# An attention, feed-forward and routing kernel: another order in the first layer with floors and key scaling on GpSimd, the widest scores computed by rows, and the second layer's output norm weight folded away with the routing in three parts

## The chip, the cores and the metric

The kernel is one program on one core of a Trainium2 chip. The metric is the device time of one execution in microseconds. Before the change it is 578.08 us, the median of 3 runs (577.95 to 581.03).

## The reference

The input `x` is 16 batches of 128 tokens of 128 features, all fp32. Two layers are added to it in turn. Cut to what matters:

```python
# layer 1: cosine attention, 16 heads of 64 queries, one head of keys and values, a learned null key
xn = ln(x, g_norm)
q = l2norm(xn @ Wq) * q_scale                      # l2norm floors the norm
k = l2norm([null_k ; (xn @ Wkv)[:, :64]]) * k_scale
v = [null_v ; (xn @ Wkv)[:, 64:]]
sim = 8 * q @ k.T + rel_pos_bias                   # causal and masked by key
x = x + ffn(ln(softmax(sim) @ v @ Wout, g_out))    # dense FFN: ln, ternary W1, gelu, ln, ternary W2
# layer 2: the same shape of attention without l2norm, with a bias given as input
h = ln(softmax(q @ k.T + bias) @ v @ Wo, g_out)
logits = h @ gate_w.T + gate_b                     # 8 experts
p, idx = top_k(softmax(logits), 2)
# each choice c: token t goes to row idx*320 + (its place among the tokens of that expert), dropped from 320 on
y[t] = sum over c of p[t,c] * keep[t,c] * (relu(xbuf[e] @ W1[e] + b1[e]) @ W2[e] + b2[e])
x = x + y
```

## The kernel before, in words

The program is written by hand, engine by engine: each of PE, ACT, DVE, POOL and SP has its own list of instructions, and semaphores order them across engines. There is no scheduler: on an engine, what stands first waits first, and everything behind it waits too. `over` walks the 16 batches in pairs (some batches written out, the rest in a loop); `attention_first` is the walk of layer 1 and `attention_second` that of layer 2, once for each engine.

A batch's 128 queries are four units of 32. Unit `u` needs only the keys up to its own end: 33, 65, 97 and 129 columns with the null key. For a unit and a batch PE multiplies queries by keys (`scores`, L888), DVE adds bias and mask and takes the negated row maximum (`biased`, L1590, four instructions, one for each pair of heads), ACT takes the exponential and the row sum (`weights`, L1296, four), DVE divides (`divide`, L1599 and L1605), PE turns the probabilities (`turn_pair` L895 and L897 for units 0 and 1, `turn_probs` L906 for 2 and 3), ACT copies them out of PSUM (`pair_T` L1303, `weights_T` L1309), and PE multiplies them by the values (`values_pair` L914 and L915 for units 0 and 1; `values` L924 for units 2 and 3, in column tiles of 128 rows by 64 columns, two side by side). DVE copies the result out (`outputs`, L1617), and PE projects it (`project`, L943, 8 matmuls). Scores lie in `psS`, two banks, each unit but the last in one; unit 3 takes both banks, 258 columns in each:

```python
if u == UNITS - 1:
    return psS[:, 1 - h, 0:2 * w]
```

Its second matmul waits until DVE has read unit 2. Both matmuls have 128 rows: the keys `kk` hold the 64 rows of a head twice, padded with zeros, so that two heads share a matmul.

In layer 1 the queries and keys of the next batch are made meanwhile: PE projects (`project_values` L838, `project_heads` L843), ACT squares (`squares`, L1263 for the keys, L1265 for the queries), DVE sums (`sum_squares`), floors (`floored`, L1576), POOL takes the power -1/2 (L584, output `qrn`), DVE scales keys (`keys_in`, L1563) and queries (`queries_norm`, L1581), PE turns them (`turn_keys` L866, `turn_queries` L872, half 0 and 1), ACT copies them back (`queries` L1279, `keys_T` L1289 and L1290). POOL also adds bias and mask for the next batch (`mask_bias`, L637) and the null value (`values_set`, L620).

In layer 2 each batch ends in the output norm: DVE reads `psA` (`out_stats` L1624, `out_read` L1638), POOL gives the reciprocal root, DVE centres and scales 136 columns, the 128 of the token and 8 raw logits (`centre` L1654 and L1656, `rescale` L1661). Groups of tokens (`GROUPS`: most batches, then two, then the last three) are routed: logits (`route_logits`, L1898), exponential (ACT, L1387), the two largest (`route_top`, L1909 to L1915), shares (`route_share`, L1923 to L1927), positions by matmul on PE (`positions`, L954) and slots (`route_slots`, L1935 to L1945). POOL scatters each tile's rows by an indirect DMA (`scatter`, L649), two of a tile, into two slot arrays. SP loads the slots of the first two experts when both arrays are complete (`load_slots`, L485), and the experts run.

## Time and profile before

| | |
|---|---|
| median of 3 runs | 578.08 us |
| the profiled execution | 581.05 us |
| its span in the trace | 579.3 us |
| mean granted clock of TensorE | 0.938 of full speed |
| busiest engine | PE, 84% of the span |

The profiled execution is the slowest of those shown, 3.0 us above the median. In the trace, the layer-1 attention runs from about 45 to 218 us, the dense feed-forward to 267, the layer-2 attention to 450, the last scatters and loads to 472, the experts to 555, the return of their rows to the end. A row of the timeline is a run of instructions on one engine: start, time to the end of the last, engine, line, operation, tiles, count, and in brackets the idle time ahead of it with what ended it. A row of the chain is a piece of the chain of work that ended last: start, time, what. A row by form is a group of instructions: count, busy time and mean ns of one, then the idle time ahead of them with what ended it. A row by stretch gives the stretch and its length, then busy time (and instructions) of PE, PE's weight loads, DVE, ACT and POOL, the granted clock, the DMA share and GB/s.

### The profile page before, as it was taken

The numbers are of one execution on the slowest core, as the hardware profiler recorded it, in microseconds if no ns is written. First come the engines' busy times: TensorE is split into PE (matmuls) and PEld (weight loads), VectorE is DVE, ScalarE is ACT, GpSimd is POOL, SyncE is SP. The second block draws the span as 40 slices with busy tenths as digits, with TensorE's granted clock in tenths as the row PEclk, the third lists the DMA queues.
The fourth block names the chain that finished last, engine by engine and source line by source line (L and its number), as shares of the span: only waits on it lengthen the run. The fifth ranks groups of instructions, "written<-read, shape, count | busy, mean of one in ns | idle before, by whom it ended". The sixth has DMA issues, their size and how long they took to land.

```text
span 579.3 us, 13792 instructions
## 1 busy us (share of the span) xinstructions
PE 485.3 (84%) x3220; PEld 391.4 (68%) x3220; DVE 422.1 (73%) x2148; ACT 375.2 (65%) x1475; POOL 303.6 (52%) x368
## 2 busy tenths in 40 slices
PE   2778999999999889979899999989778139999930
PEld 1456777777777676758688888868666127878730
DVE  3889999999999896877978888887796503343413
ACT  1568889888888876747798888967763004344410
POOL 4486666665646724775353343425766512555650
PEclk9779999999999999989999999999978759999975
DMA  5451016721100000000111210000111121323117
GB/s 166 97 182 24 20 26 130 152 78 44 43 5 5 9 4 2 0 1 9 45 42 44 79 42 8 5 6 21 33 39 40 36 64 36 85 56 83 35 39 217
DMA packets 54696, 29.73 MB, mean 51 GB/s; under 512 B 19884, under 2 KB 51572, under 8 KB 54644
## 3 DMA queue, kind: packets, MB, share of 16 engines
q1 hardware_dynamic: 48900, 22.09, 15.6%
q0 software_dynamic: 2560, 4.90, 2.7%
q10 hardware_dynamic: 3184, 2.16, 1.2%
q8 instruction: 18, 0.29, 0.2%
q14 instruction: 34, 0.28, 0.2%
HBM read 16.13 MB, written 10.90 MB: 47 GB/s over the span
## 4 chain that ended last, share of the span: by engine, by line
PE 58%; issue 11%; DVE 9%; POOL 7%; ACT 7%; DMA 5%; SPq 1%; ACTq 0%; DVEq 0%; POOLq 0%
PE psS L888 10%; PE psA L943 8%; PE psS L1193 6%; PE psT L906 5%; PE psO L924 4%; PE psQ L843 4%; PE psQ L859 4%; PE psQ L1183 3%; ACT sc L1296 2%; PE psO L914 2%; DVE sc L1590 2%; PE psO L915 2%; DMA slot_rows<-Y,dest_u 2%; ACT qT L1279 2%; PE psA L1183 1%
## 5 line engine op out<-in xcount | busy, mean ns | idle before, releaser
L1296 ACT ACTIVATE sc<-sc,negmax 128x97 f32<-128x97 f32 (+3 forms) x512 | 179.0, 354 | 26.0 <-DVE negmax L1590 25.5
L637 POOL TENSOR_TENSOR wide_buf<-bias,mask 128x132 f32<-128x132 f32 (+3 forms) x128 | 100.2, 799 | 97.5 <-DVE pn L1605 84.0
L888 PE MATMUL psS<-kk,qT 128*128 128x194 f32 (+3 forms) x512 | 102.1, 321 | 7.9 <-DVE negmax L1590 7.8
L1590 DVE CUSTOM_DVE_ANT_0 sc<-psS,wide_buf 128x97 f32<-128x97 f32 (+3 forms) x512 | 93.6, 238 | 17.5 <-PE psS L888 13.1
L888 PEld LDWEIGHTS psS<-kk,qT 128*128 128x128 f32 x512 | 79.6, 194 | 28.6 <-issue 25.1
L1296 ACT ACTIVATION_READ_ACCUMULATOR sc<-sc,negmax 128x1 f32 x512 | 97.6, 191 | 0.0
L584 POOL TENSOR_TENSOR qrn<-qssc,half 128x9 f32<-128x9 f32 (+1 forms) x32 | 55.5, 1735 | 41.8 <-DVE qssc L1576 41.7
L1605 DVE TENSOR_TENSOR pn<-sc,rsum 128x128 f32<-128x128 f32 (+3 forms) x128 | 64.9, 507 | 6.0 <-DVE rsum L1599 0.2
L943 PE MATMUL psA<-Wo,OT 128*128 128x128 f32 (+1 forms) x512 | 66.4, 285 | 0.8 <-DVE OT L1617 0.8
L943 PEld LDWEIGHTS psA<-Wo,OT 128*128 128x128 f32 x512 | 63.8, 199 | 1.8 <-DVE OT L1617 1.2
L1617 DVE TENSOR_SCALAR OT<-psO,cols 128x512 f32<-128x512 f32 x64 | 47.6, 744 | 2.6 <-PE psO L924 1.8
L906 PE MATMUL psT<-ident,pn 128*96 128x128 f32 (+1 forms) x256 | 39.8, 279 | 11.6 <-issue 10.9
L906 PEld LDWEIGHTS psT<-ident,pn 128*96 128x96 f32 (+1 forms) x256 | 28.4, 137 | 25.0 <-issue 24.6
L1590 DVE DVE_READ_ACCUMULATOR2_ANT negmax<- 128x1 f32 x512 | 41.8, 82 | 0.1
L1309 ACT COPY PT<-psT 96x512 f32<-96x512 f32 x64 | 36.7, 573 | 7.6 <-PE psT L906 7.0
L779 POOL DMA_INDIRECT choice_rows<-hT,tags x24 | 22.5, 939 | 35.5 <-ACT hT L1441 23.1
L649 POOL DMA_INDIRECT slot_rows<-Y,dest_u x32 | 32.1, 1005 | 16.2 <-DMA slot_rows<-Y,dest_u 7.5
L843 PE MATMUL psQ<-Wq,xnT 128*128 128x512 f32 x64 | 37.1, 668 | 1.0
L1279 ACT ACTIVATE qT<-psQ 128x512 f32<-128x512 f32 x64 | 34.7, 588 | 3.6 <-PE psQ L872 3.2
L924 PE MATMUL psO<-PT,vp 96*64 96x256 f32 (+1 forms) x256 | 34.8, 392 | 2.5 <-issue 1.5
L2025 DVE TENSOR_SCALAR hm<-psQ,cols 128x320 f32<-128x320 f32 x16 | 8.8, 551 | 35.0 <-PE psQ L1183 35.0
L779 POOL DMA_INDIRECT choice_rows<-qn,tags x24 | 22.5, 939 | 16.6 <-DMA choice_rows<-qn,tags 7.2
(298 smaller groups left out, 1009.7 us busy)
## 6 DMA issues: line engine op xcount, KB each, us to landing
slot_rows<-empty SPq DMA_DIRECT2D x2, 1390.0 KB, 10.5
xb<-slot_rows SPq DMA_DIRECT2D x16, 139.0 KB
vp_u<-vp SPq DMA_DIRECT2D x128, 8.0 KB, 1.7
choice_rows<-zero_row SPq DMA_DIRECT2D x8, 256.0 KB, 3.1
wide_buf<-choice_rows SPq DMA_DIRECT2D x8, 256.0 KB, 5.2
vp_u<-vp SPq DMA_DIRECT2D x64, 16.0 KB, 1.8
eW<-in_L_ffn_W SPq DMA_DIRECT2D x4, 256.0 KB, 3.0
gT<-in_L_ffn_W SPq DMA_DIRECT2D x4, 256.0 KB, 3.3
```

The lines of the kernel that those rows point to most:

```text
L584: pool.tensor_tensor(dst, src, half[:, 0:k], ALU.pow).then_inc(done, count)
L637: pool.tensor_tensor(unit_masked(i, u).rearrange("p h e k -> p (h e) k"), unit_bias(layer, u).rearrange("p h e k -> p (h e) k"), mask[laye ...
L843: pe.matmul(psQ[:, h, :], xnT[i][:], Wq[0][:, 512 * h:512 * (h + 1)], start=True, stop=True).then_inc(s["q_psum"], 1)
L888: m = pe.matmul(score_bank(u, h), qT[i][:, h, u].rearrange("p m q -> p (m q)"), kk[i][:, :, 0:w], start=True, stop=True)
L906: m = pe.transpose(psT[0:k, probs_bank(u, i), g * P:(g + 1) * P], pn[u][:, g, :], ident[:])
L924: m = pe.matmul(psO[DH * e:DH * (e + 1), 2 * P * (u - 2):2 * P * (u - 1)], vp[i][0:k, :], PT[u - 1][0:k, :, e, :], start=True, stop=True)
L943: m = pe.matmul(psA[:, Y_AT[layer]:4 * P], OT[i][:, j].rearrange("p u q -> p (u q)"), Wo[layer][:, j, :], start=(j == 0), stop=(j == 7))
L1279: act.activation(qT[i][:, h].rearrange("p u m q -> p m u q"), v, ACT.Copy, scale=1.0 if layer == 0 else DH ** -0.5).then_inc(s["q_ready"], 1)
L1296: m = act.activation(v, v, ACT.Exp, bias=negmax[:, u, g:g + 1], scale=-1.0, accum_out=psum_row[:, u, g:g + 1])
L1590: dve.tensor_tensor_reduce(sc[u][:, h, e, :], score_bank(u, h)[:, e * WIDTH[u]:(e + 1) * WIDTH[u]], unit_masked(i, u)[:, h, e, :], -1.0, - ...
L1605: dve.tensor_tensor(pn[u][:], sc[u][:].rearrange("p h e k -> p (h e) k")[:, :, 1:k + 1], rsum[:, u, :].unsqueeze(2).broadcast_to([P, 4, k] ...
L1617: dve.tensor_scalar(OT[i][:, :, 2 * half_of:2 * half_of + 2, :], v, cols[:, C_VN:C_VN + 1], None, ALU.add).then_inc(s["out_ready"], 1)
```

## The change

1. **Scores of unit 3 by rows, in both layers.** Instead of two matmuls of 128 rows by 258 columns there are four of 64 rows by 129 columns, one for each half of the array's rows and each pair of heads. Their two banks are now told apart by the half (`score_part`), all four wait until unit 2 is read, and DVE and ACT take them in another order (`in_order`).
2. **Layer 1's order.** PE: `project_heads(b + 1, 0)` comes first in a batch, and `turn_queries(b + 1, 0)` moves from the end of batch `b` to a place ahead of its unit 3. ACT: the squares of the next queries come first, the keys' squares are an instruction of their own, and the copies of the queries' halves are apart. DVE: `biased` of unit 3 moves from the next batch to the end of its own.
3. **Floors and keys on GpSimd.** `floored` and `keys_in` leave DVE; POOL floors just ahead of its power. The keys' and queries' weights and the factor 8 become a column `k_col`, by which ACT scales in `keys_T`.
4. **Layer 2's norm.** `centre` and `rescale`, three DVE instructions a batch, become `finish`, two. The weight `g_out` of layer 2 moves into `rows_T` of the experts, as a scale of ACT's copy, and the gate's column sum into its weights ahead of layer 2 (`gate_total`, `gate_centred`).
5. **Routing in three parts.** `route_slots` becomes `route_positions` and `route_slots`, and shares, positions and slots of the first group move to later batches.
6. **GpSimd's late batches.** From batch 12 of layer 2 on, all four `mask_bias` come ahead of the scatters and wait for nothing, and one scatter moves from inside the last batch to behind it.
7. **The end of layer 2.** PE turns and multiplies the last unit ahead of `project` of batch 14, `project` of batch 15 writes into a bank of its own, DVE's order follows, and the loads of slots are split: SP's queue loads the first choice's, ACT's the second's.

Three of the loads that spread a row over all partitions are gone from SP's queue.

```diff
+        def y_at(layer, b):
+            if layer == 1 and no(b, NB - 1):
+                return psS[:, 0, 0:P + EXPERTS]
+            return psA[:, Y_AT[layer]:4 * P]
...
+        def score_part(u, h, e):
             w = WIDTH[u]
             if u == UNITS - 1:
-                return psS[:, 1 - h, 0:2 * w]
-            return psS[:, u % 2, 2 * w * h:2 * w * (h + 1)]
+                return psS[:, 1 - e, w * h:w * (h + 1)]
+            return score_bank(u, h)[:, e * w:(e + 1) * w]
+        def in_order(u):
+            return [(0, 0), (1, 0), (0, 1), (1, 1)] if u == UNITS - 1 else [(0, 0), (0, 1), (1, 0), (1, 1)]
...
# SP, after the second layer's walk
-            for c in range(TOPK):
-                sp.wait_ge(s[f"slots_out{c}"], 16 * NB)
-            load_slots(0, 0)
-            load_slots(1, 1)
+            sp.wait_ge(s["slots_out0"], 16 * NB)
+            load_choice(sp, 0, 0, 0)
+            load_choice(sp, 1, 1, 0)
+            sp.wait_ge(s["slots_out1"], 16 * NB)
...
# POOL
+                apart(pool, (s["ss_step"], 2 * b + h + 1))
+                pool.tensor_scalar(qssc[:, lo:hi], qss[:, lo:hi], 1e-24, None, ALU.max).then_inc(s["q_floor"], 1)
+                pool.wait_ge(s["q_floor"], 2 * b + h + 1)
                 rsqrt(qrn[:, lo:hi], qssc[:, lo:hi], hi - lo, s["rn_ready"])
+            def keys_in(b, i):
+                pool.wait_ge(s["v_read"], b + 1)
+                pool.wait_ge(s["rn_ready"], 2 * b + 1)
+                held(pool, s["kT_psum"], b - 1)
+                pool.tensor_tensor(kd[i][:], kvs[:, 0:DH].unsqueeze(1).broadcast_to([P, 2, DH]),
+                                   qrn[:, 0:1].unsqueeze(2).broadcast_to([P, 2, DH]), ALU.mult).then_inc(
+                    s["k_ready"], 1)
...
             def attention_second():
                 def batch(b, i):
+                    late = isinstance(b, int) and b >= NB - 4
                     if not no(b, NB - 1):
-                        pool.wait_ge(s["probs_ready"], 4 * (b + NB) + 1)
-                        for u in range(UNITS - 1):
+                        if not late:
+                            pool.wait_ge(s["probs_ready"], 4 * (b + NB) + 1)
+                        for u in range(UNITS if late else UNITS - 1):
                             mask_bias(1, b + 1, u, 1 - i)
...
# PE, scores
-                      (s["scores_ready"], 4 * (n - u) if u < 2 else 4 * (n - 1)))
+                      (s["scores_ready"], 4 * (n - u) if u < 2 else 4 * (n - 1) if u == 2 else 4 * n))
+                if u == UNITS - 1:
+                    for h in range(2):
+                        for e in range(2):
+                            rows_of = slice(DH * e, DH * (e + 1))
+                            m = pe.matmul(score_part(u, h, e), qT[i][rows_of, h, u].rearrange("p m q -> p (m q)"),
+                                          kk[i][rows_of, e, 0:w], start=True, stop=True)
...
# PE, end of layer 2
-                project(1, NB - 2, 0, False)
                 turn_probs(B, 3, 1)
                 values(B, 1)
+                project(1, NB - 2, 0, False)
...
# ACT, keys_T
+                    m = act.activation(kk[i][half_of, e, 1:P + 1], psA[half_of, k0:k0 + P], ACT.Copy,
+                                       scale=k_col[half_of, 0:1] if layer == 0 else 1.0)
...
# ACT, a batch of layer 1
-                    queries(0, b, i)
+                    if not last:
+                        squares(b + 1, 0)
+                    queries(0, b, i, (1,))
+                    if not last:
+                        square_keys(b + 1)
                     if not first:
                         pair_T(b - 1, 1 - i)
-                    if not last:
-                        squares(b + 1, 0)
...
                     weights(4 * b + 1, 1)
+                    if not last:
+                        queries(0, b + 1, 1 - i, (0,))
                     weights(4 * b + 2, 2)
...
# DVE
+            def finish(b, i):
                 dve.wait_ge(s["o_rstd"], b + 1)
+                dve.tensor_scalar(Y[:, b, 0:P], Y[:, b, 0:P], o_mv[:, i, 0:1], o_rs[:, i:i + 1], ALU.subtract,
+                                  ALU.mult)
+                dve.scalar_tensor_tensor(lg[:, bass.ds(b, 1), :].rearrange("p t e -> p (t e)"),
+                                         Y[:, b, RAW_AT:RAW_AT + EXPERTS], o_rs[:, i:i + 1], gate_b[:], ALU.mult,
+                                         ALU.add).then_inc(s["n_step"], 1)
...
                     divide(b, 1)
+                    biased(n + 3, 3, i)
...
-                            if u == 3:
-                                route_share(g)
+                        if u == 1 and (no(b, NB - 5) or last):
+                            route_share(1 if last else 0)
                         if u == 2 and no(b, NB - 5):
-                            route_slots(0, 1)
+                            route_positions(0, 1)
                         if u == 1 and last:
-                            route_slots(1, 0)
+                            route_positions(1, 0)
+                        if u == 1 and (no(b, NB - 4) or last):
+                            route_slots(1 if last else 0)
```

What the change moves is seen in the order of the instructions. On PE, in layer 1, from unit 2 of batch 2 to the first turning of batch 3 (`qn` are the normalised queries, `pn` the probabilities, `kd` the keys), the order before is:

```order
L888 MATMUL psS<-kk,qT 128x194 x2
L924 MATMUL psO<-PT,vp 64x256 x4
L888 MATMUL psS<-kk,qT 128x258 x2
L832 MATMUL psA<-ident,xn 128x128
L866 MATMUL psA<-ident,kd 128x128
L872 MATMUL psQ<-ident,qn 128x128 x4
L895 MATMUL psT<-ident,pn 128x128
L897 MATMUL psT<-ident,pn 128x128 x2
L872 MATMUL psQ<-ident,qn 128x128 x4
L838 MATMUL psA<-Wkv,xnT 128x128
L843 MATMUL psQ<-Wq,xnT 128x512
L906 MATMUL psT<-ident,pn 96x128 x4
```

and with the change:

```order
L928 MATMUL psS<-kk,qT 128x194 x2
L906 MATMUL psQ<-ident,qn 128x128 x4
L964 MATMUL psO<-PT,vp 64x256 x4
L923 MATMUL psS<-kk,qT 128x129 x4
L864 MATMUL psA<-ident,xn 128x128
L900 MATMUL psA<-ident,kd 128x128
L935 MATMUL psT<-ident,pn 128x128
L937 MATMUL psT<-ident,pn 128x128 x2
L877 MATMUL psQ<-Wq,xnT 128x512
L906 MATMUL psQ<-ident,qn 128x128 x4
L870 MATMUL psA<-Wkv,xnT 128x128
L946 MATMUL psT<-ident,pn 96x128 x4
```

The first turning of the queries moved ahead of the values, the projection of the heads (128x512) ahead of the second turning, and the wide scores became four narrow ones.

On POOL, in a batch of layer 1, before:

```order
L584 TENSOR_TENSOR qrn<-qssc,half 128x9
L584 TENSOR_TENSOR rstd<-ve,half 128x6
L584 TENSOR_TENSOR qrn<-qssc,half 128x8
L620 TENSOR_TENSOR vp<-kvs,vnull 128x64
L637 TENSOR_TENSOR wide_buf<-bias,mask 128x132
```

and with the change:

```order
L628 TENSOR_SCALAR qssc<-qss 128x9
L598 TENSOR_TENSOR qrn<-qssc,half 128x9
L637 TENSOR_TENSOR kd<-kvs,qrn 128x128
L598 TENSOR_TENSOR rstd<-ve,half 128x6
L628 TENSOR_SCALAR qssc<-qss 128x8
L598 TENSOR_TENSOR qrn<-qssc,half 128x8
L645 TENSOR_TENSOR vp<-kvs,vnull 128x64
L662 TENSOR_TENSOR wide_buf<-bias,mask 128x132
```

Two floors and the keys' product joined POOL's list, each ahead of a power or of the values.

On PE, at the end of layer 2, behind the last scores, before:

```order
L906 MATMUL psT<-ident,pn 96x128 x4
L914 MATMUL psO<-PT,vp_u_1 128x128 x2
L915 MATMUL psO<-PT,vp_u_1 128x256
L943 MATMUL psA<-Wo,OT 128x136 x8
L906 MATMUL psT<-ident,pn 128x128 x4
L924 MATMUL psO<-PT,vp 64x256 x4
```

and with the change:

```order
L946 MATMUL psT<-ident,pn 96x128 x4
L954 MATMUL psO<-PT,vp_u_1 128x128 x2
L955 MATMUL psO<-PT,vp_u_1 128x256
L946 MATMUL psT<-ident,pn 128x128 x4
L964 MATMUL psO<-PT,vp 64x256 x4
L984 MATMUL psA<-Wo,OT 128x136 x8
```

The projection of batch 14 moved behind the last batch's turning and values.

## Rows read from the trace of the kernel before

**Rows 1.** Busy time of each engine, layer 1 from the first projection to the last.
```profile
56.41:205.51 149.10, 145.10 (x945) 110.85 (x944) 136.21 (x713) 129.20 (x555) 94.03 (x103) 1.00 0.23 50
```

**Rows 2.** Chain that ended last, layer 1, the first and the last projection.
```profile
56.41 1.79 PE psA L943 x16
...
205.51 1.79 PE psA L943 x16
```

**Rows 3.** PE's timeline, one batch of layer 1.
```profile
101.55 0.63 PE L906 MATMUL psT<-ident,pn 128*128 128x128 f32 x4
...
107.76 0.60 PE L872 MATMUL psQ<-ident,qn 128*128 128x128 f32 x4
...
108.81 1.12 PE L843 MATMUL psQ<-Wq,xnT 128*128 128x512 f32 x2
...
113.17 0.63 PE L906 MATMUL psT<-ident,pn 128*128 128x128 f32 x4 [0.16 <-issue]
```

**Rows 4.** ACT's timeline in the same batch.
```profile
108.15 1.09 ACT L1279 ACTIVATE qT<-psQ 128x512 f32<-128x512 f32 x2
109.12 0.49 ACT L1303 COPY PT<-psT 128x384 f32<-128x384 f32 x1
...
109.97 0.60 ACT L1265 ACTIVATE qsq<-psQ 128x512 f32<-128x512 f32 x1 [0.23 <-PE psQ L843]
110.46 0.39 ACT L1296 ACTIVATE sc<-sc,negmax 128x129 f32<-128x129 f32 x1
...
112.00 0.56 ACT L1309 COPY PT<-psT 96x512 f32<-96x512 f32 x1
```

**Rows 5.** Chain that ended last: layer 1 by its first three rows, then layer 2.
```profile
104.63 1.01 PE psO L924 x8
105.65 1.07 PE psS L888 x4
...
111.71 0.86 PE psQ L843 x2
...
375.75 0.26 PE psA L832
376.02 0.87 PE psS L888 x4
376.89 0.11 PE psT L895
```

**Rows 6.** POOL's groups by form, whole span.
```profile
L584 POOL TENSOR_TENSOR qrn<-qssc,half 128x9 f32<-128x9 f32 x16 | 28.8, 1803 | 8.6 <-DVE qssc L1576 8.6
...
L637 POOL TENSOR_TENSOR wide_buf<-bias,mask 128x132 f32<-128x132 f32 x32 | 15.9, 498 | 41.3 <-DVE pn L1605 39.5 <-issue 1.8
```

**Rows 7.** DVE's groups by form, whole span.
```profile
L1590 DVE CUSTOM_DVE_ANT_0 sc<-psS,wide_buf 128x129 f32<-128x129 f32 x128 | 29.6, 285 | 5.4 <-PE psS L888 5.3
...
L1661 DVE TENSOR_SCALAR Y<-centred,o_rs 128x136 f32<-128x136 f32 x10 | 5.6, 558 | 0.1
...
L1563 DVE SCALAR_TENSOR_TENSOR kd<-kvs,qrn,kqs 128x128 f32<-128x128 f32 x16 | 5.4, 340 | 0.1
...
L1576 DVE TENSOR_SCALAR qssc<-qss 128x9 f32<-128x9 f32 x16 | 3.1, 197 | 0.1
```

**Rows 8.** DVE's timeline, layer 2, the batch behind the first scatters.
```profile
405.65 0.23 DVE L1556 COPY kvs<-psA 128x64 f32<-128x64 f32 x1 [1.90 <-POOL vp L620]
```

**Rows 9.** PE's timeline, end of layer 2, the projection of batch 14.
```profile
442.79 3.45 PE L943 MATMUL psA<-Wo,OT 128*128 128x136 f32 x16
```

**Rows 10.** DVE's timeline, end of layer 2, the last group's two largest.
```profile
447.45 0.31 DVE L1909 MAX8 top<-le 128x8 f32<-128x8 f32 x3 [2.11 <-ACT le L1387]
```

**Rows 11.** POOL's timeline, the first and the last of the last ten scatters.
```profile
452.62 1.03 POOL L649 DMA_INDIRECT slot_rows<-Y,dest_u  x1 [1.81 <-DVE Y L1945]
...
465.53 0.96 POOL L649 DMA_INDIRECT slot_rows<-Y,dest_u  x1 [0.30 <-DMA slot_rows<-Y,dest_u]
```

**Rows 12.** SP's queue, the loads of the first two experts' slots.
```profile
467.98 4.50 SPq L485 DMA_DIRECT2D xb<-slot_rows  x8
```

More of the change, by code:

```diff
@@ L1260, in squares, with square_keys, queries @@
                 held(act, s["ss_step"], 2 * b)
[L1261 to L1263 removed]
                 act.wait_ge(s["q_psum"], 2 * b + h + 1)
[L1265 to L1268 removed]
+                m = act.activation(qsq[:, 1 + 8 * h:9 + 8 * h, :], psQ[:, h, :].rearrange("p (h d) -> p h d", d=DH),
+                                   ACT.Square)
+                if h:
+                    m.then_inc(s["sq_ready"], 1)
+            def square_keys(b):
+                act.wait_ge(s["kv_psum"], b + 1)
+                act.activation(qsq[:, 0, :], psA[:, P:P + DH], ACT.Square).then_inc(s["sq_ready"], 1)
+            def queries(layer, b, i, halves=(0, 1)):
                 B = b + NB * layer
                 held(act, s["scores_psum"], 4 * B - 4)
[L1271 removed]
+                for h in halves:
                     if layer == 0:
@@ L1328, in batch @@
                     weights(4 * b + 1, 1)
+                    if not last:
+                        queries(0, b + 1, 1 - i, (0,))
                     weights(4 * b + 2, 2)
@@ L1344, in attention_first @@
                 ternary_abs()
+                input_T(0, 1, 1)
+                queries(0, 0, 0, (0,))
                 keys_T(0, 0, 0)
-                input_T(0, 1, 1)
                 over(act, NB, batch, 2, 2)
@@ L1691, in batch @@
                         outputs(b - 2, 1, i, True)
-                    if not first:
-                        biased(n - 1, 3, 1 - i)
                     if first:
@@ L1717, in batch @@
                         out_stats(0, b - 2, i)
-                    if not last:
-                        floored(b + 1, 1)
                     biased(n + 2, 2, i)
@@ L1722, in batch @@
                         moments(b - 2, i)
-                    if not last:
-                        keys_in(b + 1, 1 - i)
-                    else:
+                    if last:
                         dense_stats(1)
```

204 lines of the change are left out of this document (96 added, 108 removed).

## The prediction

> **What bounds the kernel now.** I read the busy time by stretch first. In layer 1, from the first projection to the last, PE is busy 145.1 of 149.1 us, DVE 136.2, ACT 129.2 and GpSimd 94.0, at the full clock [rows 1]. PE sets the pace, DVE (91%) stands close behind, and GpSimd has a third to spare. The chain of waits says how long a batch is: the first and the last of its projections lie 149.1 us apart [rows 2], which is 13 batches of 11.47 us.
>
> Then I read one batch on PE and on ACT. PE turns unit 2 at 101.55, the queries' second half at 107.76 and unit 3 at 113.17 [rows 3]: two parts of 6.21 and 5.41 us. In the second part ACT works with 0.23 us of waiting: it copies the queries' halves from 108.15, the pair from 109.12, squares from 109.97, takes unit 3's exponentials from 110.46, and copies unit 2's turned probabilities from 112.00 [rows 4]. ACT alone would hold that part at its length. That decides the largest term below.
>
> Late in layer 2 the reading changes: DVE waits for GpSimd, which scatters ahead of the next values [rows 8], and behind the last scores the chain runs through the routing, ten scatters and the first loads of slots [rows 9 to 12].
>
> **The scores by rows.** No row of this trace has matmuls of 64 rows. The nearest are the column tiles of the values: eight records of 256 columns in 1.01 us [rows 5], where the scores, four full records of 258 columns, take 0.87 in layer 2 [rows 5]. Eight at that price would be 1.74, so the column tiles run two at a time. A record of 128 columns takes 0.11 (the turning at 376.89). What goes into another tile mode costs more: the scores take 1.07 behind column tiles, 0.20 more than the 0.87 behind a full matmul, and the input's turning behind column tiles takes 0.26, not 0.11, so 0.15 [rows 5]. The new visit has eight records of 129 columns. Side by side that is 4 x 0.11 + 0.20 + 0.15 = 0.79, say 0.80: 0.27 less in layer 1, 0.07 less in layer 2. One after another it is 8 x 0.11 + 0.35 = 1.23; with a weight load of the same length ahead of each it is 8 x 0.22 + 0.35 = 2.11. I take side by side, as the column tiles show it. All four now wait until DVE has read unit 2; before, only the second matmul did. Behind them on PE stand the turnings of the input, the keys and the pair, and for these ACT waits; the values ahead of the scores (1.01) cover the wait.
>
> The Trainium skill's page "TensorEngine Tiling (Array Packing)", under Key Properties, says that different tiles load and multiply in parallel, and that a change of mode drains the engine. By the first half the visit is the 0.80 above, by the second both switches are paid, and the sum stands; no run here shows it for tiles of rows yet.
>
> **Layer 1's order.** The second part has PE waiting at the projection of the heads: 1.12 us [rows 3], against 0.86 for the same two matmuls where nothing waits [rows 5]. The new order projects the heads first and takes that 0.26 away. But ACT's list is as long as it was. From the moment the heads are there: squares 0.49 (109.97 to 110.46), the queries' half 0.49 (half of the 0.97 from 108.15 to 109.12), pair and key squares 0.62 (109.12 to 109.74), exponentials of unit 3 1.54 (110.46 to 112.00), and 1.17 from there to PE's turning [rows 3, 4]. With 0.86 + 0.23 (the projection and ACT's wait behind it) ahead, that is 5.40, as the 5.41 before. So this part keeps its length, and only the first one shrinks: 6.21 - 0.27 = 5.94. Moving the turning of the queries and biasing unit 3 earlier lets ACT start its exponentials a little sooner; for that I add 0.08, an estimate between nothing and the 0.23 of ACT's wait [rows 4]. A batch loses 0.35, and 13 batches **-4.6**. The bounds are 0 (PE waits for what it gained) and -13 (1.0 a batch: 0.27, the 0.26, and the two 0.23 waits of ACT, once each for both parts).
>
> **Floors and keys on GpSimd.** DVE loses 2 x 0.20 and 0.34 a batch [rows 7]. GpSimd gains them: nearest rows are its sum of 132 columns, 0.50, and its power of 9 columns, 1.80 [rows 6]. Two floors at 0.2 to 1.8 and a product of 0.50 make 0.9 to 4.1 a batch; GpSimd had 55.1 us free in 13 batches [rows 1], 4.2 each. Beside other work in either case: **0**. The chain from the sums to the turned keys gets longer by 0.2 to 1.8, and the keys are turned at the end of the batch.
>
> **Start and end of layer 1.** Three loads and two products go from the setup, one column joins: 0, give or take 1. At the end unit 3's bias of batch 15, four of about 0.28 [rows 7], less what it already overlaps, comes ahead of the last divide: **+0.7**, between 0 and 1.1.
>
> **Layer 2, ten batches.** PE gives 0.07 a batch. DVE's norm drops one of three instructions, the one of 0.56 [rows 7]; DVE is not the bound, so I count 0.08 of it. -0.15 each, **-1.5**, between 0 and -3.5 (the 0.07 and half of the 0.56).
>
> **Late batches.** DVE waits 1.90 for GpSimd's values behind four scatters [rows 8], and once more like it a batch later. In the new list the masks go ahead of the scatters without waiting, so scatters and values start sooner; the scatters themselves take as long. Shares and slots leave the batch that is fullest. I take 3.0 of the 3.8 us: **-3.0**, between -1 and -4.5 (both waits and 0.7 for the routing that moved).
>
> **The end.** PE projects batch 14 for 3.45 us [rows 9] ahead of the last turning; now it doesn't. DVE waits 2.11 for the exponential of the last routing, as ACT takes it behind unit 3's work [rows 10]. With the unit turned sooner, the first of the ten scatters, at 452.62 [rows 11], comes between 2.1 and 3.45 sooner; their pace, 12.9 us for nine steps [rows 11], does not change. I take 2.8. The eight loads take 4.50 us on one queue [rows 12], 0.56 each; over two queues the first expert's four are out two steps sooner, up to 1.1; I take 0.6. Together **-3.4**, between -2.1 and -4.6. ACT issues its four behind the last exponential, and behind them on ACT stand only the copies that need the loaded rows. The experts keep their price: a copy with a scale for a copy.
>
> **Sum.** -4.6 + 0.7 - 1.5 - 3.0 - 3.4 = -11.8. The profiled execution took 581.05 us (span 579.3), so 569.25; the median of the runs is 578.08, 0.5% below it, which gives 566.3, **566 us**. About 0.5% (2.9 us) is what a measurement of this kernel can tell from no change.
>
> **The rivals** (all against the median).
>
> - *ACT gives way and PE alone bounds layer 1.* The batch loses 1.0, 8.4 us more than forecast over 13 batches: 558. For it: the new order feeds ACT earlier. Against it: ACT had only 0.23 of waiting there [rows 4], and its work is the same.
> - *DVE sets the pace of layer 1.* It was busy 136.2 of 149.1 [rows 1], and loses 0.74 a batch; if the places where it must answer PE (unit 2 read ahead of all four scores, where before the first of two didn't wait) eat the gain, layer 1 stands where it was: 4.6 less gain, 571. The Trainium skill's same page, under PSUM Bottleneck, says that tiling speeds up TensorE but not the emptying of PSUM; by that rule this rival would be the forecast. The rows speak for it with DVE's 91% and against it with the 0.74 that leave DVE.
> - *The row tiles run one after another.* A visit is 1.23: layer 1 then gains 0.08 - 0.16 = 0.08 worse a batch (+1.0), layer 2 loses 0.36 - 0.08 = 0.28 a batch (+2.8); with the rest, +1.0 + 0.7 + 2.8 - 3.0 - 3.4 = -1.9: 576, no change that can be told.
> - *The slower side: weight loads stand open between the row tiles.* Each of the eight records waits for its own load, 2.11 a visit. Layer 1 loses 2.11 - 1.07 - 0.08 = 0.96 a batch (+12.5), layer 2 2.11 - 0.87 - 0.08 = 1.16 (+11.6), and with the other terms +19.1: 597. It turns to slower as soon as a visit costs over about 1.35. For it: PE's loads were busy 110.9 us of layer 1 [rows 1], so they are not far from the matmuls. Against it: the column tiles, with as many loads, show none of it [rows 5].
> - *The change does not do what it says.* A wait put wrongly could keep the old order in time; the order of the instructions shows it done.
>
> **Chances.** Forecast 0.54 (its own range 561 to 571, from the bounds of the sum), PE alone 0.12, DVE 0.15, one after another 0.10, open loads 0.08, nothing changed 0.01. The range 555 to 576 leaves out the open loads, the slower half of the tiles one after another and the edges of the first three. Faster: the first three, less 0.02 for the third, 0.79. Same: tiles one after another, the 0.02 and the 0.01, 0.13. Slower: 0.08.
>
> **What would show it.** Right: projections of layer 1 about 11.1 apart; the four narrow scores starting in pairs and taking about 0.8 with their switches; the heads at 0.86; the waits of 1.90 at the values' copy gone; the first of the last ten scatters about 3 us nearer to the last scores. Wrong: the distance still 11.47, with PE waiting at unit 3's scores for DVE (the second rival), or the eight records following each other by 0.11 (the third) or 0.22 (the fourth); or powers on GpSimd ending after PE has reached the keys' turning, which would price the floors above the range.

## The result, and the profile after

The changed kernel takes 583.42 us (median of 6 runs, 580.84 to 586.44), the kernel before 578.10 in the same set: the ratio is 1.0077, 95% interval 1.0048 to 1.0105. It is slower by 0.8% where 2% faster was forecast, and outside the range. The profiled execution took 586.44, the slowest of the six (span 584.7); differences of stages below are taken against the profiled execution before (581.05, span 579.3), which was also the slowest of its runs. Medians below leave out one run in the slower state in each of three versions (594.95, 728.47 and 634.80 us).

Layer 1 in the changed kernel, by busy time from the first projection to the fourteenth (as in [rows 1]), and the chain there (as in [rows 2]):

```profile
56.12:207.86 151.74, 141.98 (x996) 108.44 (x996) 131.66 (x675) 131.75 (x555) 105.44 (x142) 1.00 0.21 49
```

```profile
56.12 1.79 PE psA L984 x16
...
207.86 1.79 PE psA L984 x16
```

PE has 3.1 us less work than before and DVE 4.5 less, ACT has 2.5 more, and the same 13 batches take 151.74 us instead of 149.10. The busiest engine, PE, is now idle for 9.8 us where it was for 4.0: no engine is full, and a ring of waits over several engines sets the pace (a ring: each waits for the one ahead of it, and the first for the last). PE's timeline of one batch shows where PE stands (as in [rows 3]):

```profile
94.82 0.72 PE L923 MATMUL psS<-kk,qT 64*128 64x129 f32 x8
95.47 0.33 PE L864 MATMUL psA<-ident,xn 128*128 128x128 f32 x1
...
96.59 1.12 PE L877 MATMUL psQ<-Wq,xnT 128*128 128x512 f32 x2 [0.36 <-ACT xnT L1302]
97.55 0.60 PE L906 MATMUL psQ<-ident,qn 128*128 128x128 f32 x4
...
99.09 0.63 PE L928 MATMUL psS<-kk,qT 128*128 128x66 f32 x4 [0.28 <-ACT qT L1329]
```

The scores by rows do run side by side: eight records in 0.72 us where 0.80 was forecast; in the trace they start in pairs, 0.01 us apart in a pair and 0.11 from pair to pair. They do not wait for DVE here. But the heads, now first in the batch, wait for ACT's copy of the input, and unit 0's scores wait for ACT's copy of the queries. The chain of the same batch shows why the copy of the input is late:

```profile
92.78 0.68 PE psS L928 x4
...
94.73 1.23 ACT sc L1352 x7
...
96.08 0.38 ACT xnT L1302
96.46 0.14 issue
96.59 1.14 PE psQ L877 x2
...
98.25 0.60 ACT qT L1329
```

From unit 2's scores the chain goes over DVE's bias to ACT's exponentials of unit 2 (`sc`), and the copy of the input (`xnT`) stands behind these. Neither unit 3's scores nor the copies of the keys stand in the chain, in this batch or anywhere from 56 to 208 us.

Late in layer 2 three timelines (DVE, GpSimd, PE) belong together:

```profile
410.68 0.23 DVE L1621 COPY kvs<-psA 128x64 f32<-128x64 f32 x1 [2.17 <-POOL vp L645]
...
411.60 3.00 DVE L1656 TENSOR_TENSOR pn<-sc,rsum 128x512 f32<-128x512 f32 x1
```

```profile
404.97 1.24 POOL L674 DMA_INDIRECT slot_rows<-Y,dest_u  x1 [3.06 <-DVE Y L1987]
...
410.24 0.34 POOL L645 TENSOR_TENSOR vp<-kvs,vnull 128x64 f32<-128x64 f32 x1
...
411.07 2.98 POOL L662 TENSOR_TENSOR wide_buf<-bias,mask 128x132 f32<-128x132 f32 x4
```

```profile
414.70 1.09 PE L946 MATMUL psT<-ident,pn 128*128 128x128 f32 x4 [3.57 <-issue]
415.58 3.83 PE L984 MATMUL psA<-Wo,OT 128*128 128x136 f32 x16
```

A wait for GpSimd's values is still there (2.17, as in [rows 8]); the second one, a batch later, is gone. The scatters ahead of these values did not start sooner, as the first of them waited 3.06 us for DVE's slots. Then DVE's division of 512 columns takes 3.00 us: it ends at 414.60, 0.55 behind the last of GpSimd's four mask sums. PE stands 3.57 us, and then its clock is granted at half (1.2 GHz; the mean of the stretch from 410 to 430 is 0.83 of full speed): the projection takes 3.83 where it takes 2.02 at full clock.

The same fall of the clock stands at the start of layer 2, where before there was none, behind the longer wait of unit 3's scores (PE's timeline, before and after):

```profile
283.27 0.67 PE L888 MATMUL psS<-kk,qT 128*128 128x258 f32 x2 [1.15 <-DVE negmax L1590]
...
285.02 1.95 PE L859 MATMUL psQ<-xnT,Wq 128*128 128x128 f32 x16
```

```profile
288.25 1.23 PE L923 MATMUL psS<-kk,qT 64*128 64x129 f32 x8 [1.57 <-DVE negmax L1641]
...
290.96 3.60 PE L893 MATMUL psQ<-xnT,Wq 128*128 128x128 f32 x16
```

The end of layer 2 does what was forecast (as in [rows 10, 11], DVE, GpSimd and PE):

```profile
452.70 0.30 DVE L1948 MAX8 top<-le 128x8 f32<-128x8 f32 x3 [0.29 <-ACT le L1449]
```

```profile
458.35 1.03 POOL L674 DMA_INDIRECT slot_rows<-Y,dest_u  x1 [0.45 <-DVE Y L1987]
...
471.31 0.95 POOL L674 DMA_INDIRECT slot_rows<-Y,dest_u  x1 [0.30 <-DMA slot_rows<-Y,dest_u]
```

The wait of 2.11 is 0.29. The last scores of unit 3 begin at 445.85 and the ten scatters 12.5 us behind them; before it was 437.75 and 14.9.

**Where the time went**, by the starts of the projections in PE's timeline, before and after (us):

| stretch | before | after | difference |
|---|---|---|---|
| start to the first projection | 56.25 | 55.95 | -0.3 |
| 13 batches of layer 1 | 149.09 | 151.75 | +2.7 |
| its last two projections | 15.59 | 18.20 | +2.6 |
| feed-forward, to layer 2's first projection | 68.90 | 71.17 | +2.3 |
| eight batches of layer 2 | 82.23 | 81.12 | -1.1 |
| the batch with the first routing | 12.98 | 11.07 | -1.9 |
| four late batches | 47.79 | 52.04 | +4.2 |
| from there to the end | 146.5 | 143.4 | -3.1 |

### The profile page after: what moved, and what is told of

It reads as the page before. It is cut to its first block, busy times and chain, and to the rows that moved or that the text cites. A ratio compares the mean times of both kernels' runs of the same rounds, so it can differ in the third digit from the quotient of the medians.

```text
span 584.7 us, 13956 instructions
## 1 busy us (share of the span) xinstructions
PE 486.0 (83%) x3348; PEld 391.6 (67%) x3348; DVE 408.5 (70%) x2073; ACT 381.5 (65%) x1475; POOL 318.9 (55%) x416
## 4 chain that ended last, share of the span: by engine, by line
PE 60%; issue 10%; DVE 9%; ACT 8%; DMA 5%; POOL 5%; SPq 1%; DVEq 0%; ACTq 0%; POOLq 0%
PE psA L984 9%; PE psS L928 8%; PE psS L1240 6%; PE psQ L877 5%; PE psT L946 5%; PE psQ L893 4%; ACT sc L1352 4%; PE psQ L1230 3%; DVE sc L1641 3%; PE psO L954 3%; PE psO L964 2%; PE psO L955 2%; PE psS L923 2%; DMA slot_rows<-Y,dest_u 2%; PE psA L1230 1%
## 5 line engine op out<-in xcount | busy, mean ns | idle before, releaser
L662 POOL TENSOR_TENSOR wide_buf<-bias,mask 128x132 f32<-128x132 f32 (+3 forms) x128 | 98.8, 794 | 89.7 <-DVE pn L1656 85.7
L928 PE MATMUL psS<-kk,qT 128*128 128x130 f32 (+2 forms) x384 | 66.9, 296 | 8.1 <-DVE negmax L1641 4.2
L1656 DVE TENSOR_TENSOR pn<-sc,rsum 128x128 f32<-128x128 f32 (+3 forms) x128 | 67.3, 526 | 5.8
L928 PEld LDWEIGHTS psS<-kk,qT 128*128 128x128 f32 x384 | 57.7, 194 | 20.0 <-issue 19.2
L984 PE MATMUL psA<-Wo,OT 128*128 128x128 f32 (+1 forms) x496 | 65.2, 287 | 0.0
L984 PEld LDWEIGHTS psA<-Wo,OT 128*128 128x128 f32 x496 | 62.1, 200 | 0.6 <-issue 0.4
L598 POOL TENSOR_TENSOR qrn<-qssc,half 128x9 f32<-128x9 f32 (+1 forms) x32 | 56.9, 1778 | 2.7
L946 PE MATMUL psT<-ident,pn 128*96 128x128 f32 (+1 forms) x256 | 41.1, 285 | 10.3 <-issue 9.1
L1365 ACT COPY PT<-psT 96x512 f32<-96x512 f32 x64 | 36.9, 576 | 15.8 <-PE psT L946 14.9
L1329 ACT ACTIVATE qT<-psQ 128x512 f32<-128x512 f32 x64 | 36.0, 588 | 13.9 <-PE psQ L906 13.8
L893 PE MATMUL psQ<-xnT,Wq 128*128 128x128 f32 x256 | 32.8, 284 | 0.0
```

Source lines behind the costliest of these rows:

```text
L598: pool.tensor_tensor(dst, src, half[:, 0:k], ALU.pow).then_inc(done, count)
L662: pool.tensor_tensor(unit_masked(i, u).rearrange("p h e k -> p (h e) k"), unit_bias(layer, u).rearrange("p h e k -> p (h e) k"), mask[laye ...
L893: m = pe.matmul(psQ[:, h, j * P:(j + 1) * P], Wq[1][:, (4 * h + j) * P:(4 * h + j + 1) * P], xnT[i][:], start=True, stop=True)
L928: m = pe.matmul(score_bank(u, h), qT[i][:, h, u].rearrange("p m q -> p (m q)"), kk[i][:, :, 0:w], start=True, stop=True)
L946: m = pe.transpose(psT[0:k, probs_bank(u, i), g * P:(g + 1) * P], pn[u][:, g, :], ident[:])
L984: m = pe.matmul(y_at(layer, b), OT[i][:, j].rearrange("p u q -> p (u q)"), Wo[layer][:, j, :], start=(j == 0), stop=(j == 7))
```

## The experiments

All ratios are to the kernel before, run on the same chip in the same set, with 95% intervals. The first set undoes one part each, and does one alone.

**Mask waits back.**

```diff
-                    late = isinstance(b, int) and b >= NB - 4
+                    late = False
```

> The changed kernel with one thing undone: in layer 2's batches from 12 on, GpSimd's mask sums wait again for the division of the unit ahead and stand on both sides of the scatters. Theory: without those waits the sums (2.98 us at 411.07) run beside DVE's division of the same time, which took 3.00 us where it takes 0.69, PE then stood 3.57 us and ran 6.8 us at half clock; with the waits back the division takes about 0.7 everywhere, the low clock there goes, and 4 to 6 us come back: 578 to 579. Rival: the division was slow for another reason, or the scatters merely wait elsewhere: 582 to 584.

580.57 us, 1.0035 (1.0012 to 1.0057). In its DVE timeline the division of the same batch takes 0.69 again:

```profile
410.54 0.69 DVE L1656 TENSOR_TENSOR pn<-sc,rsum 128x512 f32<-128x512 f32 x1
```

PE's wait ahead of the turning is 1.09, and the low clock at 414 is gone: four late batches take 45.23 instead of 52.04. The collision is shown, though the run gained 2.9 us by the medians, 2.4 by the ratios, and not 4 to 6. The Trainium skill's page "SBUF — State Buffer", under Who interferes with whom, says that a DVE instruction with two inputs in SBUF contends with a GpSimd instruction that reads SBUF, over ports that only one of them holds at a time; the 3.00 beside the 2.98 agree, and I had not weighed that section.

**Old order, with the rest of the change.** PE, ACT and DVE of layer 1 as before:

```diff
-                    if not last:
-                        project_heads(b + 1, 0, 1 - i)
                     turn_queries(b, 1)
                     if not last:
                         project_values(b + 1, 1 - i)
+                        project_heads(b + 1, 0, 1 - i)
...
                     divide(b, 1)
-                    biased(n + 3, 3, i)
...
```

> The changed kernel with layer 1's order undone on PE, ACT and DVE (heads, queries' turning, squares, copies and the bias of unit 3 where they were before); floors and keys stay on GpSimd and the scores by rows stay. Theory: the new order puts the queries' copy ahead of unit 2's exponentials on ACT and the heads behind the input's copy, and gives back what the scores by rows gain; undone, a batch of layer 1 takes about 11.2 instead of 11.65 us, 13 batches 5 to 6, and the end of layer 1 starts without a fall of the clock: 576 to 578. Rival: floors on GpSimd or the wait for unit 2 hold layer 1; then a batch stays above 11.5 and the time at 583.

588.25 us, 1.0163 (1.0115 to 1.0211): slower still, so my theory fell. A batch takes 11.89. (This undo left the keys' squares behind the queries' on ACT, which was not so before.)

**Full scores, with the rest of the change.**

```diff
-                        for e in range(2):
-                            rows_of = slice(DH * e, DH * (e + 1))
-                            m = pe.matmul(score_part(u, h, e), qT[i][rows_of, h, u].rearrange("p m q -> p (m q)"),
-                                          kk[i][rows_of, e, 0:w], start=True, stop=True)
+                    m = pe.matmul(bank, qT[i][:, h, u].rearrange("p m q -> p (m q)"),
+                                  kk[i][:, :, 0:w], start=True, stop=True)
...
```

> The changed kernel with the scores of unit 3 again as two matmuls of 128 rows, of which only the second waits for unit 2. Theory: a visit by rows takes 0.65 us instead of 1.07 to 1.16, so without it PE is busy 0.4 longer in layer 1 and 0.2 to 0.4 in layer 2; as layer 1 is now held by ACT's order, only part shows: 584 to 589. Rival: waiting for all of unit 2 costs what the rows save (PE stood 1.57 at the start of layer 2 and lost its clock); then 580 to 583.

585.98 us, 1.0103 (1.0069 to 1.0136), as the theory had it. A batch takes 11.95: in the new order the rows are worth 0.28 a batch.

**Rows alone, on the kernel before.**

> The kernel before with one part of the change: the scores of unit 3 by rows, in both layers. Theory: side by side a visit takes about 0.65 instead of 1.07 in layer 1 and 0.87 in layer 2; a batch of layer 1 loses 0.3 to 0.45 and one of layer 2 0.1 to 0.2: 571 to 574. Rival: the wait of all four matmuls for unit 2 eats it, as DVE stands close behind PE: 577 to 580, with PE waiting for DVE ahead of these scores.

579.63 us, 1.0014 (0.9991 to 1.0037): the rival. Its chain in a batch of layer 1:

```profile
103.72 0.68 PE psS L903 x4
...
105.51 0.09 DVE negmax L1606
105.61 0.14 issue
105.74 0.72 PE psS L898 x8
```

From the end of unit 2's scores (104.40) to that of unit 3's (106.46) it takes 2.06 us; before, from 104.63 to 106.72 [rows 5], 2.09. PE's timeline has the scores wait 0.34 for DVE's last read of unit 2. The 0.35 that the rows save (0.72 for 1.07) goes into that wait. In layer 2 eight batches take 10.20 each instead of 10.28.

A second set took the floors back to DVE, once in the new order and once in the old, and made only half of the scores wait for unit 2.

**Floors on DVE, new order, mask waits back.**

```diff
-                pool.tensor_scalar(qssc[:, lo:hi], qss[:, lo:hi], 1e-24, None, ALU.max).then_inc(s["q_floor"], 1)
...
+                dve.tensor_scalar(qssc[:, lo:hi], qss[:, lo:hi], 1e-24, None, ALU.max).then_inc(s["q_floor"], 1)
...
```

> The changed kernel with GpSimd's mask waits back (as in the first run, 580.57 us) and, beyond that, floors and the keys' scaling back on DVE; layer 1's new order and the scores by rows stay. Theory: with the old order, scores by rows and floors on DVE a batch of layer 1 takes 11.4 us, with floors on GpSimd 11.83, so the move to GpSimd costs 0.4 a batch in the chain from the sums to the normalised queries, and the new order gives half of it back; with floors on DVE the new order shows its gain: a batch about 11.2, 13 batches 5 to 6 less: 575. Rival: in the new order the batch is a ring of heads, squares, exponentials, division and projection that holds neither floors nor keys; then it stays at 11.6 and the time at 580 to 581.

579.60 us, 1.0021 (0.9997 to 1.0045), a batch of 11.64 against 11.67: the rival. Floors and keys on GpSimd cost nothing that can be told, as forecast.

**Old order and floors on DVE** (the two undos together, mask waits back).

> The changed kernel without its layer 1 parts: old order, floors and keys on DVE, mask waits back. What stays of the change is the scores by rows, the norm folded in layer 2, the routing in three parts and the end of layer 2. Theory: layer 1 as in the run with the scores by rows alone (11.4 a batch), the first scatters' batch about 1.9 shorter, the end about 2.7 shorter: 579.63 less 4 to 5, so 575. Rival: the feed-forward between the layers and the falls of the clock behind it take that back: 578 to 580.

581.83 us, 1.0050 (1.0023 to 1.0078). A batch stayed at 11.89, though only the column scale on ACT and the place of the keys' squares were left of layer 1's change beside the rows. The time is above both ranges. That pointed to ACT.

**Only half of the scores wait.**

```diff
-                    for h in range(2):
-                        for e in range(2):
+                    for e in range(2):
+                        if e == 1:
+                            apart(pe, (s["scores_ready"], 4 * n))
+                        for h in range(2):
```

> The changed kernel with mask waits back (580.57 us), and the four matmuls of unit 3's scores in another order: both of the upper half's rows first, into the bank that unit 2 does not use, without waiting for unit 2, then both of the lower half's behind the wait. The two halves then no longer run side by side. Theory: where PE waited 1.57 us for unit 2 at the start of layer 2 it waits about 1.1, and its clock falls less often; a visit costs 1.2 instead of 0.65, which layer 1 does not feel, as its batches are not held by PE; layer 2 feels 0.3 to 0.5 in ten batches: 581 to 584. Rival: the falls of the clock hang on that wait more than on anything else: 577 to 579.

579.62 us, 1.0011 (0.9989 to 1.0033), against 580.57: within the spread. A visit in layer 1 still took 0.72, not 1.2, so the halves ran side by side in this order too. At the start of layer 2 PE stood only 0.94 ahead of the second half, and the clock fell all the same (the projection behind it took 3.62). So that one wait's length does not decide the fall.

The third set, with ACT's list restored, led to the version that beats both kernels.

**Old order with the keys' squares first** (scaled copies and GpSimd's floors stay).

> The changed kernel with mask waits back, layer 1's old order, and now also the keys' squares ahead of the queries' on ACT as before; floors and keys stay on GpSimd, and ACT still scales in the copies of the keys (0.36 us each where a plain copy took 0.26). Theory: the 11.8 a batch of the two runs in the old order came from ACT, which squared the keys (0.22) behind its wait for the heads and not within it, and from the scaled copies (0.2 a batch), not from GpSimd: a batch takes about 11.6, 0.2 above the run with the scores by rows alone. Rival: the floors and the keys on GpSimd are late; then it stays near 11.8.

583.15 us, 1.0060 (1.0034 to 1.0087), a batch of 11.79: the rival's number. That floors and keys on GpSimd are its cause is not shown by it; the last pair of runs speaks against that.

**Layer 1 of before with rows; layer 2 changed, with mask waits.**

```diff
-                    m = act.activation(kk[i][half_of, e, 1:P + 1], psA[half_of, k0:k0 + P], ACT.Copy,
-                                       scale=k_col[half_of, 0:1] if layer == 0 else 1.0)
+                act.copy(kk[i][0:DH, 0, 1:P + 1], psA[0:DH, k0:k0 + P])
+                act.copy(kk[i][DH:P, 1, 1:P + 1], psA[DH:P, k0:k0 + P]).then_inc(s["kk_ready"], 1)
```

> Layer 1 of the kernel before, but with the scores by rows, and layer 2 of the changed kernel with mask waits back: floors and keys on DVE with the product of the keys' and queries' weights, plain copies of the keys, old order. Theory: layer 1 takes 11.4 a batch as in the run with the scores by rows alone (579.63), the first scatters' batch is 1.9 shorter, ten batches of layer 2 about 0.15 each, the end about 2.7, less 1 for the scaled copies of the experts' rows: 574 to 576. Rival: the clock falls between the layers and at the end take it back: 578 to 580.

577.57 us, 0.9979 (0.9950 to 1.0009): between the two, and not clear of no change. A batch takes 11.53.

**The same with full scores.**

> As the run with layer 1 of the kernel before and layer 2 of the changed one, but with unit 3's scores as two full matmuls, of which only the second waits for unit 2. Theory: PE is not what holds a batch of layer 1, so the full scores cost nothing there, about 0.1 in each of ten batches of layer 2; and PE's stop of 1.57 at the start of layer 2 becomes 1.15 again, behind which the clock did not fall before, worth 2 to 3: 572 to 574, the best so far. Rival: the clock does not depend on it, and the rows are worth their 1 to 3: 576 to 578.

575.99 us, 0.9945 (0.9922 to 0.9967): faster than either kernel, though the time is just under the rival's range and not in the theory's. The 1.6 us between this run and the one by rows are not clear of the spread; what differs is seen in the profiles. The two end layer 1 like this, by rows and then full (PE's timeline):

```profile
209.72 0.72 PE L913 MATMUL psS<-kk,qT 64*128 64x129 f32 x8
212.00 0.30 PE L925 MATMUL psT<-ident,pn 128*128 128x128 f32 x1 [1.57 <-issue]
...
213.30 3.55 PE L974 MATMUL psA<-Wo,OT 128*128 128x128 f32 x16
```

```profile
209.66 1.14 PE L913 MATMUL psS<-kk,qT 128*128 128x258 f32 x4
212.13 0.30 PE L920 MATMUL psT<-ident,pn 128*128 128x128 f32 x1 [1.33 <-issue]
...
213.42 2.05 PE L969 MATMUL psA<-Wo,OT 128*128 128x128 f32 x16
```

The faster scores end sooner, the turning starts about when it did, PE stands 1.57 instead of 1.33, and the projection behind it runs at half clock: 3.55 for 2.05. From the last projection of layer 1 to the first of layer 2 it is 71.63 by rows and 68.97 with full scores. The mean granted clock points the same way over all runs and not only in the profiled ones: its median is 0.943 in the kernel before and in the version with full scores, and 0.934 by rows.

**PE's wait filled.** Twelve turnings that nothing reads, at each of two places of the version by rows:

```diff
+                if layer == 1 and no(b, 3):
+                    for _ in range(12):
+                        pe.transpose(psA[:, 0:P], xn[:, i, :], ident[:])
...
+                    else:
+                        for _ in range(12):
+                            pe.transpose(psQ[:, 0, 0:P], ident[:], ident[:])
                     turn_pair(b, i)
```

> The run with layer 1 of the kernel before and the scores by rows (577.57 us), with 12 turnings added that nothing reads, at the two places where PE waits longest behind these scores: ahead of the last turning of layer 1 (waits 1.57 us) and ahead of unit 3's scores in the second batch of layer 2 (about 1.6). They fill the wait with 1.3 us of PE's work and delay nothing. Theory: by rows the scores end sooner, PE stands longer, and behind these two waits its clock falls to half (3.55 for the projection that takes 2.05); filled, the falls at 213.6 and 285 us go and 3 to 4 us come back: 573 to 575. Rival: the falls come from something else, such as the work of the stage as a whole, or the added work delays the chain: 577 to 579.

578.03 us, 0.9976 (0.9957 to 0.9996): the rival's time. But the two falls went (PE's timeline, at the first place):

```profile
210.54 1.53 PE L1037 MATMUL psQ<-ident 128*128 128x128 f32 x12
212.18 0.30 PE L928 MATMUL psT<-ident,pn 128*128 128x128 f32 x1
...
213.48 2.05 PE L977 MATMUL psA<-Wo,OT 128*128 128x128 f32 x16
```

The last two projections of layer 1 take 15.73 instead of 17.35 and the feed-forward 68.70 instead of 71.63, 4.5 us together. So it is the standing of PE, and not the rows' own work, behind which the clock falls there. The same wait does not always bring the fall: in the run with the old order PE stood 1.58 at the start of layer 2, and the projection behind it took 1.95. And the median did not move. In the profiled execution, which was the slowest of this run's twelve (580.60), a scatter waited 2.36 us for an earlier one to land, PE stood 3.06 from 404, and the clock fell at 408, 428 and 439. In the median of the twelve the mean granted clock is 0.937, against 0.934 without the turnings and 0.943 with full scores, so the clock fell elsewhere instead; where, in a median execution, was not tried.

**Masks ahead, in the best version.**

> The best run so far (layer 1 of before, full scores, layer 2 of the changed kernel with mask waits, 575.99 us) with that one part of the change put back: GpSimd's masks of the late batches ahead of the scatters and without waiting. Theory: DVE's division of 512 columns meets the masks and takes up to 3 us instead of 0.69, a batch there takes 14.5 instead of 12.2, and the clock may fall behind it: 2 to 5 us more, 578 to 581. Rival: it was a meeting of that layer 1's timing alone; then 575 to 577.

576.85 us, 0.9953 (0.9931 to 0.9976): the rival's time, within the spread of 0.9945. But the meeting is there, so its reason was wrong: the division takes 3.00 again (at 404.56, masks of 2.97 at 404.04), and that batch takes 14.44 instead of 12.16 in the profiles. What it costs the median of this version is not shown.

A last pair put back the two suspects of layer 1, each alone, in the best version.

**Scaled copies alone.**

> The best run (layer 1 of before, full scores, 575.99 us) with one part of the change put back in layer 1: the keys' and queries' weights as a column by which ACT scales in its copies of the keys, instead of a product on DVE. Floors and keys' product stay on DVE. Theory: each of the two copies takes 0.36 us instead of 0.26, they stand in ACT's chain ahead of the queries' copies, and a batch of layer 1 goes from 11.55 to about 11.75: 578 to 579. Rival: it was the floors and keys on GpSimd that made the run in the old order slow; then the batch stays at 11.55 and the time at 576.

579.39 us, 1.0015 (0.9994 to 1.0036). A batch goes from 11.55 to 11.80. The copies on ACT, in the changed kernel and in the one before (groups by form; layer 2's copies, without a column, are the second row):

```profile
L1343 ACT ACTIVATE kk<-psA,k_col 64x128 f32<-64x128 f32 x32 | 11.5, 358 | 2.2 <-DVE k_col L1815 2.0
L1343 ACT ACTIVATE kk<-psA 64x128 f32<-64x128 f32 x32 | 8.7, 272 | 9.8 <-DVE kvs L1621 5.1 <-issue 4.5
```

```profile
L1290 ACT COPY kk<-psA 64x128 f32<-64x128 f32 x32 | 8.3, 260 | 0.4
```

A column as scale adds 0.1 us to each copy, and in the old order both stand in the chain, ahead of the queries' copy and the heads (the chain of this run):

```profile
109.00 0.04 ACT kk L1320
109.05 0.32 issue
109.36 0.36 ACT kk L1320
109.73 0.02 issue
109.75 0.61 ACT qT L1306
110.36 0.14 issue
110.49 1.10 PE psQ L863 x2
```

The Trainium skill's page "ScalarE: Activation LUTs", under What ACT_TABLE_LOAD costs, gives about 93 ns for each pointer operand of 128 by 1; the 0.358 against 0.260 agree, and I had not weighed that either.

**New order alone.**

> The best run with one part of the change put back in layer 1: the new order on PE, ACT and DVE. Full scores, floors, the keys' product and plain copies as in the kernel before. Theory: the new order closes a ring through the heads' projection, ACT's squares and queries, PE's scores, turning and projection, unit 2's bias and exponentials and the input's copy, in which full scores of unit 3 stand too; a batch takes about 11.9, and the time is 580 to 582. Rival: the order is what gains, and only the scaled copies hid it: a batch below 11.4 and 572 to 574.

580.15 us, 1.0029 (1.0008 to 1.0050). A batch goes from 11.55 to 11.84, and the stretch from the thirteenth projection of layer 1 to its last from 26.76 to 30.17 us. Its chain runs through PE and ACT's copy of the input, on which the heads now wait:

```profile
107.27 1.07 PE psS L913 x4
108.34 0.11 PE psA L854
...
108.73 0.38 ACT xnT L1287
109.11 0.04 issue
109.15 1.12 PE psQ L867 x2
```

Layer 1 in nine of the kernels, from the starts of the first and the thirteenth projection in PE's timeline (the difference by 12 is a batch):

| order | scores | copies | floors | first, thirteenth | batch |
|---|---|---|---|---|---|
| old (before) | full | plain | DVE | 56.25, 194.32 | 11.51 |
| old | rows | plain | DVE | 56.19, 193.99 | 11.48 |
| old (best version) | full | plain | DVE | 56.48, 195.07 | 11.55 |
| old | full | scaled | DVE | 56.53, 198.09 | 11.80 |
| old | rows | scaled | GpSimd | 57.23, 198.69 | 11.79 |
| new | full | plain | DVE | 55.82, 197.86 | 11.84 |
| new | full | scaled | GpSimd | 56.34, 199.75 | 11.95 |
| new | rows | scaled | DVE | 56.50, 196.12 | 11.64 |
| new (the change) | rows | scaled | GpSimd | 55.95, 196.00 | 11.67 |

## Why the prediction was wrong

By the stretches the kernel came out 17.2 us behind the sum: layer 1 gave 7.3 of it, the end of layer 1 and the feed-forward 4.2, the late batches 5.3.

**Layer 1, -4.6: the step that failed; it measured +2.7.** The sum kept the second part of a batch at ACT's length and let the first shrink by all that PE's visit became shorter ("6.21 - 0.27 = 5.94"), with 0.08 more for the order. The price of the visit was right (0.72 for 0.80). Two other things were wrong.

The order, priced at -0.08, costs 0.29 alone. I took ACT's list for a length and did not follow what PE waits for in it: with the heads first, they wait for the copy of the input, which in the changed kernel stands behind unit 2's exponentials, and with full scores behind unit 3's scores.

The rows' -0.27 was worked out on the order of before, and there they give 0.02 to 0.03: the scores by rows wait for DVE's last read of unit 2, and that wait (0.34) took the 0.35 saved. That is the second rival, "eat the gain", to which I gave 0.15. In the changed kernel the rows do give 0.28, but that the number fits is luck: with full scores, unit 3's scores stand in the new order's ring, so the rows only give back most of what the order costs, and then the ring runs over DVE and ACT. The rival's sign, PE waiting at these scores for DVE, is not seen in the changed kernel.

The column scale, which the sum left out, costs 0.25 alone in the old order. In the new order it costs at most 0.11 with full scores (11.95 for 11.84, floors on GpSimd included); by rows the copies of the keys are not in the chain, and no run shows what it costs there. Floors and keys on GpSimd were right at 0.

**End of layer 1 and feed-forward, +0.7 and 0: mis-sized, +2.6 and +2.3.** Most of it is the clock: at the end of layer 1 PE stands 1.1 us longer in all, and the projection behind it takes 3.68 for 2.05. I priced PE's waits by their length and not by what PE does behind them at half clock; no row of before showed a fall at these places.

**Layer 2's batches, -0.15 each: right.** Eight took 1.11 us less, 0.14 each; the version with full scores keeps 0.12 of it, so nearly all of it comes without the rows, with the norm in the main, and does not add to the rows' 0.08.

**Late batches, -3.0: half right, then turned round, +2.3.** The batch of the first routing gave 1.9. But "the masks go ahead of the scatters without waiting" was counted as a gain only: the waits that I took for needless also kept GpSimd's sums away from DVE's division. And it did not let the scatters start sooner: the first waited 3.06 for the slots, which had moved a batch later, and four scatters stood ahead of the values as before, so that one wait of 2.17 stayed. With the mask waits back the four late batches take 45.23, 2.6 less than before; part of this is the clock, which before had fallen at 429.

**The end, -3.4: right.** Scatters 2.4 sooner behind the last scores, 3.1 in all from batch 13 to the end, loads included.

**"A copy with a scale for a copy" was wrong on the experts too**: 0.687 for the copy of 512 columns where it was 0.585. There it is hidden: from the first turning of the rows to the end it is 107.2 us before and 107.1 after.

The slower rival I named, open weight loads, did not happen; the time rose by other ways, the order, the clock and the masks. Its terms add up to +18.4 and not +19.1. The bounds of the forecast's terms, added up, run from 552 to 576, wider than the 561 to 571 that I gave as its own range.

## What to carry to other kernels

When no engine is full, follow the ring: shortening an instruction helps only if what comes next waits for that instruction last. A small cost on the engine that closes the ring weighs as much as a large saving beside it: here two copies that took 0.1 us more each cost a batch 0.25 in the old order, where 0.35 less on PE gave 0.03. A wait that looks needless may be what keeps two engines off a shared resource, so price what will run beside what once it is gone. And where the clock falls behind an engine's standing, count the standing twice: once as time, once as what runs at half speed after.

## What had not been expected of the hardware

Making PE faster made its clock lower: at the end of layer 1, by rows PE stood 1.57 us instead of 1.33 and then was granted half its clock (1.2 GHz), and 12 useless turnings brought the 2.4 GHz back at that place. A DVE division of 0.69 us took 3.00 beside GpSimd's sums.
